# A spatial mamba stage: one-hot spreads in fp32 from 32-row strips, states handled in pairs

## What is computed

```
x, z   = silu(conv4(W_in x_t) + b), silu(W_z x_t)
dt     = softplus(W_dt x + b_dt);  Bt, Ct = W_B x, W_C x      (16 values each)
h[d,n] = exp(-exp(A_log[d,n]) * dt[d]) * h[d,n] + dt[d] * x[d] * Bt[n]
y[d]   = sum_n h[d,n] * Ct[n] + D[d] * x[d];   out = W_out (y * z)
```

## Time and profile before

| | |
|---|---|
| median of 3 runs | 8825.46 us |
| the profiled execution, and its span | 8822.09 us, 8820.3 us |
| busy: TensorE, VectorE, ScalarE, GpSimd | 81%, 66%, 47%, 45% of the span |
| spatial mamba, first to last scan | 4118.9 to 6497.6 us |
| mean granted TensorE clock, whole span | 0.866 |

### The profile page before, as it was taken

How to read it: one execution, slowest core, us unless ns; L and a number is a source line. 1 busy time by engine, 2 the same in 40 slices (tenths; PEclk the granted TensorE clock), 3 DMA queues, 4 the chain that set the end, 5 groups by cost and what they waited for, 6 DMA issues and landing times. The chain is left out here.

```text
span 8820.3 us, 125816 instructions
## 1 busy us (share of the span) xinstructions
PE 7134.5 (81%) x36126; PEld 3794.4 (43%) x36126; DVE 5809.4 (66%) x6140; ACT 4130.8 (47%) x6750; POOL 3948.4 (45%) x3287
## 2 busy tenths in 40 slices
PE   8688666999997549886777777777779999999980
PEld 7366252333334414573222222222237777777760
DVE  2011025777772238313888888888879999999985
ACT  3311025666662247303555555555545555555542
POOL 0000000222220210003888888888868777778770
PEclk9788888999998779856888888888879999999995
DMA  9454435333334633432111111111100000000007
GB/s 151 131 134 129 90 103 174 99 100 101 100 100 118 208 137 102 128 89 49 36 36 36 34 32 35 36 36 35 31 21 11 10 10 10 10 10 10 10 16 190
DMA packets 793540, 639.85 MB, mean 73 GB/s; under 512 B 305947, under 2 KB 700323, under 8 KB 785691
## 3 DMA queue, kind: packets, MB, share of 16 engines
q1 hardware_dynamic: 793179, 635.26, 28.3%
HBM read 379.66 MB, written 197.82 MB: 65 GB/s over the span
## 5 line engine op out<-in xcount | busy, mean ns | idle before, releaser
L2275 POOL TENSOR_TENSOR spa_hc<-spa_hs,spa_cr 128x483 f32<-128x483 f32 x1184 | 1322.5, 1125 | 442.8 <-DVE spa_hs L2550 423.9
L2684 POOL TENSOR_TENSOR spe_hc<-spe_hs,spe_cu 128x1024 f32<-128x1024 f32 x552 | 1291.5, 2360 | 314.8 <-DVE spe_hs L2881 314.8
L2550 DVE TENSOR_TENSOR_SCAN spa_hs<-spa_p_d,spa_hs,spa_bx 128x483 f32<-128x483 f32 x1168 | 1414.8, 1217 | 0.0
L2881 DVE TENSOR_TENSOR_SCAN spe_hs<-spe_p_d,spe_bx 128x1024 f32<-128x1024 f32 x552 | 1233.9, 2275 | 110.8 <-ACT spe_p_d L2830 110.7
L2470 ACT ACTIVATE spa_p_d<-spa_p_d,spa_av 128x483 f32<-128x483 f32 x1184 | 744.8, 636 | 1004.8 <-PE spa_p_d L2335 1003.9
L2758 PE MATMUL spe_p_y<-spe_idt,spe_hc 128*128 128x128 f32 x8832 | 1041.4, 277 | 0.0
L2758 PEld LDWEIGHTS spe_p_y<-spe_idt,spe_hc 128*128 128x128 f32 x8832 | 1019.8, 194 | 0.0
L2540 DVE TENSOR_TENSOR spa_bx<-spa_br,spa_p_u 128x483 f32<-128x483 f32 x1184 | 754.5, 642 | 353.7 <-PE spa_p_u L2339 340.6
L1037 DVE TENSOR_REDUCE attention_nm<-attention_p_s 128x2 f32<-128x640 f32 x1024 | 789.3, 812 | 260.9 <-PE attention_p_s L894 259.6
L2830 ACT ACTIVATE spe_p_d<-spe_p_d 128x896 f32<-128x896 f32 x552 | 474.1, 900 | 923.5 <-PE spe_p_d L2743 923.3
L995 ACT ACTIVATE attention_pr<-attention_p_t 128x512 f32<-128x512 f32 x1280 | 710.7, 599 | 411.7 <-PE attention_p_t L917 287.8
(11 more groups left out here) (428 smaller groups left out, 12036.5 us busy)
## 6 DMA issues: line engine op xcount, KB each, us to landing
spa_pg<-spa_parts SPq DMA_DIRECT2D x888, 60.4 KB, 2.1
attention_qs<-scratch_qp SPq DMA_DIRECT2D x768, 64.0 KB, 2.7
attention_rc<-scratch_den SPq DMA_DIRECT2D x128, 256.0 KB
scratch_qp<-queries_parts SPq DMA_DIRECT2D x96, 256.0 KB, 2.3
spa_xt<-scratch_x SPq DMA_DIRECT2D x148, 121.5 KB, 2.7
scratch_spec<-spectrum_spc SPq DMA_DIRECT2D x64, 260.0 KB, 4.6
inverse_spec<-scratch_spec SPq DMA_DIRECT2D x64, 260.0 KB, 3.6
spectrum_xs<-in_x_dram SPq DMA_DIRECT2D x64, 256.0 KB, 5.2
```

The lines of the kernel that those rows point to most:

```text
L2275: nc.gpsimd.tensor_tensor(hc[:, k % 8, :], hs[:, 4 * g + q, :], cr2[:, s % 2, :], ALU.mult).then_inc(weighted, 1)
L2550: nc.vector.tensor_tensor_scan(hs[:, b, :], p_d[k % 4][:, 0:NA], bx[:, k % 4, :], first, ALU.mult, ALU.add).then_inc(scanned, 1)
L2684: nc.gpsimd.tensor_tensor(hc[:, k, :, d, :].rearrange("p s d t -> p d s t"), hs[:, k % 2, d, :, :], rows, ALU.mult)\
L2881: nc.vector.tensor_tensor_scan(hs[:, k % 2, d].rearrange("p d s t -> p (d s t)"), p_d[h][:, :], bx[:, k % 2, d].rearrange("p d s t -> p (d ...
```

## The change

The spreads are fp32 matmuls straight from the 32 partitions of du that hold the block's channels, against a one-hot matrix of 32 rows; the three bf16 parts, their copies and subtractions, the twelve transfers and the sel and pg tiles are gone, and du has two buffers. Blocks go in pairs: two strips, with one semaphore step, for dt and for u; one feed multiply for two blocks out of a two-bank tile p_u; one multiply with C for two blocks. Scans and decays stay one per block. The chunks begin 32 tokens earlier (PADX, SHIFT), so that the jump token is the last of each segment of 69. The feed tile bx has a slot for each of the 16 blocks, the jump's constant is written in its last columns once, and the feed multiply writes only the 68 other columns. So L2251, L2263 and the three extra rows are not needed. The constants get to their partitions through a small tensor in DRAM. The convolution's bias is added by ScalarE. The order lists are new. The core of the diff:

```diff
-PADX = 4
+PADX = 36
...
+SHIFT = KEPT - JUMP - 1
...
-        sel = st.sb("sel", [99, NBL, 128], BF16)
+        hot = st.sb("hot", [128, 4, 128])
...
-        du = st.sb("du", [128, 2, NA])
-        rest = st.sb("rest", [128, 2, NA])
-        parts = st.sb("parts", [128, 3, 2, NA], BF16)
-        pg = st.sb("pg", [99, 2, 2, 4, NA], BF16)
+        du = st.sb("du", [128, 2, 2, NA])
...
-        bx = st.sb("bx", [128, 4, NA])
+        bx = st.sb("bx", [128, NBL, NA])
...
-        p_u = [st.ps(f"p_u{i}", [128, 512]) for i in range(2)]
...
+        p_u = st.ps("p_u", [128, 2, 512])
...
+        def rows(t):
+            return t.rearrange("p (r w) -> p r w", w=KEPT)
         def jumps(t):
-            return t.rearrange("p (r w) -> p r w", w=KEPT)[:, :, JUMP]
+            return rows(t)[:, :, KEPT - 1]
...
+                    sp.dma_start(xt[q * C:(q + 1) * C, s, 0:NA + 3], x2[:, bass.ds(c * NA + (PADX - SHIFT - 3 - q), NA + 3)]).then_inc(x_in[s], 16)
...
+            sp.wait_ge(jump_ready, 1)
+            sp.dma_start(steady.rearrange("(d s) -> d s", s=ST), jump[:, :]).then_inc(jump_out, 16)
+            sp.wait_ge(jump_out, 16)
...
+                for q in range(4):
+                    sp.dma_start(jump2[:, 4 * q:4 * q + 4], steady.rearrange("(g q n) -> n q g", g=4, q=4)[:, q, :]).then_inc(jump_in, 16)
+            stream(sp, NC, UA, HEAD, 4, (0, next_load), (3, store))
...
+            nc.gpsimd.memset(hs[:, :, 0:SHIFT], 0.0).then_inc(zeroed, 1)
...
+                after(pool, dt_spread, (c - 1) * NP)
+                after(pool, u_spread, (c - 1) * NP)
+                d, e = du[:, s % 2, 0, :], du[:, s % 2, 1, :]
+                nc.gpsimd.tensor_tensor(d, soft[:, :], relu[:, :], ALU.add).then_inc(dt_step, 1)
...
-                nc.gpsimd.tensor_tensor(du[:, 1, :], du[:, 0, :], xz[:, s, 0, :], ALU.mult).then_inc(u_ready, 1)
...
-                nc.gpsimd.tensor_tensor(jumps(du[:, 0, :]), jumps(du[:, 0, :]), fold60[:, :], ALU.mult).then_inc(dt_step, 1)
-                nc.gpsimd.memset(jumps(du[:, 1, :]), 0.0).then_inc(u_ready, 1)
-            def remainder(c, s, r):
...
-            def lowest(c, s, r):
...
-            def fix_b(c, s, r):
...
-                nc.gpsimd.tensor_tensor(jumps(br[:, s % 2, :]), one7[:, :], one7[:, :], ALU.mult).then_inc(b_fixed, 1)
-            def weigh(k0, k1):
+                nc.gpsimd.tensor_tensor(e, d, xz[:, s, 0, :], ALU.mult).then_inc(u_ready, 1)
+                pool.wait_ge(u_ready, c + 1)
+                nc.gpsimd.tensor_tensor(jumps(d), jumps(d), fold60[:, :], ALU.mult).then_inc(dt_step, 1)
...
+            def weigh(j0, j1):
                 def run(c, s, r):
...
+                    if j0 == 0:
                         pool.wait_ge(c_copied, c + 1)
...
+                    for j in range(j0, j1):
+                        pool.wait_ge(scanned, c * NBL + (2 * j + 2))
+                        after(pool, summed, c * 4 + (j // 2 - 1))
+                        k = 2 * j
+                        nc.gpsimd.tensor_tensor(hc[:, k % 8:k % 8 + 2, :], hs[:, k:k + 2, :],
+                                                cr2[:, s % 2, :].unsqueeze(1).broadcast_to([128, 2, NA]), ALU.mult).then_inc(weighted, 1)
                 return run
...
+            stream(pool, NC, UA, HEAD, 2, (2, weigh(0, 1)), (1, step_sizes), (2, weigh(1, 6)), (0, silu), (2, weigh(6, 8)))
...
-                nc.tensor.matmul(p_x[:, 0:NA], wi[:, 1, :], xt[:, s, 1:1 + NA], start=False, stop=False)
-                nc.tensor.matmul(p_x[:, 0:NA], cr[:, :], one[:, :], start=False, stop=True).then_inc(x_done, 1)
+                nc.tensor.matmul(p_x[:, 0:NA], wi[:, 1, :], xt[:, s, 1:1 + NA], start=False, stop=True).then_inc(x_done, 1)
...
+            def spread_dt(j):
                 def run(c, s, r):
...
+                    pe.wait_ge(dt_step, 2 * c + 2)
+                    after(pe, scanned, c * NBL + (2 * j - 2))
+                    for e in range(2):
+                        g = 2 * (j % 2) + e
+                        v = slice(32 * g, 32 * g + 32)
+                        mm = nc.tensor.matmul(p_d[(2 * j + e) % 4][:, 0:NA], hot[v, j // 2, :], du[v, s % 2, 0, :], start=True, stop=True)
+                    mm.then_inc(dt_spread, 1)
+                return run
...
+            def spread_u(j):
+                def run(c, s, r):
+                    pe.wait_ge(u_ready, c + 1)
+                    after(pe, bx_ready, c * NP + j)
+                    for e in range(2):
+                        g = 2 * (j % 2) + e
+                        v = slice(32 * g, 32 * g + 32)
+                        mm = nc.tensor.matmul(p_u[:, e, 0:NA], hot[v, j // 2, :], du[v, s % 2, 1, :], start=True, stop=True)
+                    mm.then_inc(u_spread, 1)
                 return run
...
+            stream(pe, NC, UA, HEAD, 4,
+                   (2, spread_dt(0)), (2, spread_u(1)), (1, derive_dt),
+                   (2, spread_dt(1)), (2, spread_u(2)), (3, total(3)),
+                   (2, spread_dt(2)), (2, spread_u(3)), (0, project_x),
+                   (2, spread_dt(3)), (2, spread_u(4)), (3, project_out), (0, project_z),
+                   (2, spread_dt(4)), (2, spread_u(5)), (2, skip), (2, total(0)),
+                   (2, spread_dt(5)), (2, spread_u(6)), (1, derive_b), (2, total(1)),
+                   (2, spread_dt(6)), (2, spread_u(7)), (1, derive_c),
+                   (2, spread_dt(7)), (1, spread_u(0)), (2, total(2)))
...
-                nc.scalar.activation(xz[:, s, 0, :], p_x[:, 0:NA], ACT.Copy).then_inc(x_read, 1)
-                nc.scalar.activation(sg[:, 0, :], p_x[:, 0:NA], ACT.Exp, scale=-1.0).then_inc(x_read, 1)
+                nc.scalar.activation(xz[:, s, 0, :], p_x[:, 0:NA], ACT.Identity, bias=cb[:, 0:1]).then_inc(x_read, 1)
+                nc.scalar.activation(sg[:, 0, :], p_x[:, 0:NA], ACT.Exp, scale=-1.0, bias=cb[:, 1:2]).then_inc(x_read, 1)
...
-            def high(c, s, r):
...
-            def middle(c, s, r):
...
-            def decay(k0, k1):
+            def decay(j0, j1):
...
+                    for k in range(2 * j0, 2 * j1):
+                        act.wait_ge(dt_spread, c * NP + (k // 2 + 1))
+                        nc.scalar.activation(p_d[k % 4][:, 0:NA], p_d[k % 4][:, 0:NA], ACT.Exp, scale=av2[:, k:k + 1]).then_inc(decay_ready, 1)
...
+            stream(act, NC, UA, HEAD, 4, (2, decay(0, 1)), (1, softplus_in), (2, decay(1, 2)), (1, softplus_out), (2, decay(2, 3)), (0, read_x),
+                   (2, decay(3, 4)), (3, copy_out), (0, read_z), (2, decay(4, 5)), (0, sigmoid_ln), (2, decay(5, 6)), (1, copy_b),
+                   (0, sigmoid_exp), (2, decay(6, 7)), (1, copy_c), (2, decay(7, 8)))
...
+            dve.wait_ge(jump_in, 64)
+            nc.vector.tensor_copy(bx[:, :, :].rearrange("p k (r w) -> p k r w", w=KEPT)[:, :, :, KEPT - 1],
+                                  jump2[:, :].unsqueeze(2).broadcast_to([128, NBL, RA])).then_inc(w_ready, 1)
...
+            def feed(j):
                 def run(c, s, r):
...
+                    if j == 0:
+                        dve.wait_ge(b_copied, c + 1)
+                    dve.wait_ge(u_spread, c * NP + (j + 1))
+                    after(dve, scanned, (c - 1) * NBL + (2 * j + 2))
+                    def kept(t):
+                        return t.rearrange("p k (r w) -> p k r w", w=KEPT)[:, :, :, 0:KEPT - 1]
+                    b = rows(br[:, s % 2, :])[:, :, 0:KEPT - 1].unsqueeze(1).broadcast_to([128, 2, RA, KEPT - 1])
+                    nc.vector.tensor_tensor(kept(bx[:, 2 * j:2 * j + 2, :]), b, kept(p_u[:, :, 0:NA]), ALU.mult).then_inc(bx_ready, 1)
...
+            def scan(j):
+                def run(c, s, r):
+                    for k in (2 * j, 2 * j + 1):
+                        dve.wait_ge(decay_ready, c * NBL + (k + 1))
+                        if k % 2 == 0:
+                            dve.wait_ge(bx_ready, c * NP + (j + 1))
+                            after(dve, weighted, (c - 1) * NP + (j + 1))
+                        start = isinstance(c, int) and c == 0
+                        v = slice(SHIFT if start else 0, NA)
+                        nc.vector.tensor_tensor_scan(hs[:, k, v], p_d[k % 4][:, v], bx[:, k, v], 0.0 if start else hs[:, k, NA - 1:NA],
+                                                     ALU.mult, ALU.add).then_inc(scanned, 1)
...
+            order = []
+            for j in range(NP):
+                order += [(2, feed(j + 1)) if j + 1 < NP else (1, feed(0)), (2, scan(j))]
+                if j == 1:
+                    order.append((3, gate))
+            stream(dve, NC, UA, HEAD, 4, *order)
...
-    k["a_alog2"] = p("A_log").reshape(16, 8 * ST).T
+    k["a_alog2"] = p("A_log").reshape(4, 4, 8 * ST).transpose(2, 1, 0).reshape(128, 16)
...
-    merge_branches(nc, *of("ys ye x2 groups16 m_gn m_att"), out)
+    merge_branches(nc, t["ys"][:, SHIFT:SHIFT + LX], *of("ye x2 groups16 m_gn m_att"), out)
```

165 lines of the change are left out of this document (29 added, 136 removed).

## The result

The kernel after takes 8312.73 us (median of 4 runs, 8306.83 to 8323.03), the kernel before beside it 8822.75: a ratio of 0.9424 (0.9407 to 0.944). That is faster, as forecast, and faster than the range allowed (8425 to 8700). The profiled executions differ by 8820.3 - 8313.0 = 507.3 us of span.

| part of the span, us | before | after | difference |
|---|---|---|---|
| up to the first scan of spatial mamba | 4118.9 | 4112.3 | -6.6 |
| spatial mamba, first to last scan | 2378.7 | 1983.4 | -395.3 |
| between the stages | 45.4 | 45.8 | +0.4 |
| spectral mamba, first to last scan | 2027.9 | 1921.8 | -106.1 |
| the rest | 249.4 | 249.7 | +0.3 |

The account below looks back on a forecast made before the run. It took DVE's work plus its idle time behind PE's late spreads as the bound; 32.26 to 28.2 us over 74 chunks gives 300 us, with 6 for the ends 306, so 8520 us; range 8425 to 8700.

Parts of the forecast that it names:

- Nothing outside the stage: Whole program: gains were counted only for spatial mamba and its ends; the other mamba stage got no term.
- 28.2 us a chunk: Spatial mamba's steady state: chunk falls from 32.26 us to the middle between 27.05 (no idle) and 29.2 (7.5% idle).
- DVE's floor, 27.05: DVE's own work per spatial chunk: 16 scans, 8 feeds and the gate take 27.05 us, only 0.35 less than before.
- The old order's cover, 1.13 us: Spreads of u before the change: the old order gave the next feed only one scan, 1.13 us, of cover.
- The slack, 1.7 for dt and 1.1 for u, once one or two matmuls: PE's new spread order: slack of 1.7 us for dt, 1.1 for u, absorbing one or two long matmuls once.
- PE's sum: PE's work per spatial chunk at full clock: ordinary matmuls 7.2, totals 4.0, spreads 11.2, together 22.4 us.
- rival B: PE becomes the bound at a fair clock through tiling changes and spreads without overlap: 30.0 us a chunk, 8650; chance 0.13.
- The clock: PE's mean clock in the spatial stage, 0.82 before: a right forecast would show 0.85 or more.
- Rival A: 32-row spreads drop PE's clock to 1.2 GHz: 37.8 us a chunk, PE the bound, 9230 in all; chance 0.08.
- POOL 21, ACT 17 us, splitting free: Spatial chunk: POOL falls from 26.3 to about 21 us, ACT to 17, both hidden; dropping the transfers gains nothing in steady state.
- The ends: Outside the steady state: 11 us won before the first spread, 5 lost in setup for the constants, 6 net.

Follow-up runs that it names:

- before_order: Kernel before, with the spread of u for block k+1 issued behind the spread of dt for block k, still singly; ratio 0.99, 30.96 us a chunk.
- pairs_bf16: Kernel after, with spreads as bf16 matmuls of 96 rows reading a constant, without row strips or splitting; ratio 0.942, 26.83 us a chunk.
- pairs_old_order: Kernel after with bf16 spreads from a constant, and u's spread of each pair right behind dt's of that pair; ratio 1.0411, 38.71 us a chunk.
- before_no_split: Kernel before without the bf16 splitting, its copies and twelve transfers a chunk; spreads read a constant; ratio 0.9981, 32.25 us a chunk.

## Why the prediction was wrong

The kernel is faster for the kind of reason it gave, DVE's idle time behind late spreads, and its sum was short by 8520 - 8313 = 207 us, of two kinds.

- **Nothing outside the stage** (wrong, 106 us). The sum had terms for one stage only. The earlier trace rows gave the spectral stage 1664.92 us of DVE in 1800, and the prediction took its idle 7.5% for a property of such a pipeline. It was, for the most part, the stop of PE at each turn that comes with loads of code: with the code elsewhere DVE is busy 1765.25. The loss had been put at nothing, and without it the stage took 106.1 us less. The step failed twice, since that 7.5% was also the upper bound for the idle time left in the changed stage. Set against the kernel before with its code well placed (0.988), the change is worth 0.9424 / 0.988 = 0.954.
- **"28.2 us a chunk"** (wrong, about 100 us). The middle between no idle time and 7.5% was taken; there is none, DVE is busy 1700.00 of 1700.00 us. (28.2 - 26.85) x 74 = 100 us; by the table of parts the stage gave 395 us for 300.
- **DVE's floor, 27.05** (right, 0.2 high). A feed of 952 elements has 1126 ns in the records for 1135 forecast, and 1.04 us from start to start.
- **The old order's cover, 1.13 us** (wrong). The kernel before has two tiles of u, so the spread for block k waits for feed k-2, and between that and feed k stand a scan, a feed and a scan: 1.13 + 0.55 + 1.13 = 2.8 us. That is more than the 2.26 of the new order, so a longer cover for u isn't what the pairs brought. What the runs show in its place is that single blocks are slower in the chunks with a low clock (`before_order`) and pairs aren't (`pairs_bf16`). An estimate from the same rows fits that: from one release of u to the feed after the next, PE has 3 x 1.13 + 2 x 0.55 = 4.5 us singly and 4 x 1.13 + 1.05 = 5.6 with pairs, and one matmul less in its longest place.
- **The slack, 1.7 for dt and 1.1 for u, once one or two matmuls** (right in kind, small). 1.9 us are taken up in one place. Part of why it reaches further is in the timeline: when PE is late, both pairs are released and run together in 1.33 us instead of 2.03, so lateness pays itself back.
- **PE's sum** (terms mis-sized). The spreads were put at 8 x 1.4 = 11.2 us; they take 8 x 1.77 = 14.2, since in five of eight groups dt and u don't overlap. Six of the eight ordinary matmuls cost about 1.0 instead of 0.90 (in part rival B, below), so they are 7.8 for 7.2. With 4.0 for the totals the sum is 26.0 for 22.4; and 26.85 less the four short waits of PE in the chunk of the timeline (0.85 together) is 26.0 too. That is more than rival B's no-overlap figure of 25.6. It fits because the clock went to 1.00, where the prediction had asked for no more than 0.85.
- **The clock** (right in direction, cause not known). It was 0.82 where DVE and PE wait for each other, 0.88 in `before_order`, 0.74 in `pairs_old_order`, and 0.98 in `pairs_bf16`, without any strip. In these bf16 kernels it goes with how smoothly the work runs. In `before_order` the clock is already low when the matmuls of project_x start, and DVE's wait comes behind them; but PE had itself waited for DVE before that. Which of the two begins it, no run separates.
- **Rival A** (didn't happen, mechanism shown). Single strips do bring the clock to 0.56 and the kernel to 1.2022; pairs of strips on opposite rows, kept near each other, do not. 0.08 was perhaps low for a thing that shares its strips with the real kernel.
- **Rival B** (its costs are there, its end isn't). The same matmul, B's, has these groups in the kernel after, and in `pairs_bf16`, which has no strips (busy us, mean ns of one record, two to a matmul):

```profile
L2283 PE MATMUL spa_p_x<-spa_xz,spa_wbr 128*128 128x483 f32 x128 | 68.9, 620 | 0.0
```

```profile
L2290 PE MATMUL spa_p_x<-spa_xz,spa_wbr 128*128 128x483 f32 x128 | 62.3, 567 | 0.0
```

  A full matmul beside strips is 2 x 53 ns = 0.1 us dearer, by the timelines 1.01 from start to start instead of 0.90. In the kernel after the first product of x, behind strips, has 620 ns a record and the second, behind the first, 567. The Trainium skill, TensorEngine Tiling (Array Packing), Key Properties, speaks of a drain at a change of the tiling mode; this agrees with a short one. The projections of z and of the output take 1.00 and 0.95 us from start to start in `pairs_bf16` too, so of the 0.6 us a chunk some 0.5 at most is the strips', and it was hidden.
- **POOL 21, ACT 17 us, splitting free** (right). 1333.38 and 1111.43 over 1700 / 26.85 = 63.3 chunks are 21.1 and 17.6; `before_no_split` is at 0.9981, in the kernel before.
- **The ends** (the sum right by luck). 6.6 us were won up to the first scan for 6 forecast, from other terms. The first spread starts 8.7 us after the last step on du (4097.05 to 4105.79, behind the matmuls of z, B and C), not 3, so 5.7 are won there and not 11; and the constants' route cost nothing where 5 were taken: PE begins at 4078.20, against 4078.96.
